# First keys through two queues, half of their blocks on ScalarE, zero rows late, new orders of steps

## What is computed

```python
# layer 0: attention, 32 query heads over 8 key/value heads of depth 8; keys and values are the context itself
x = x + softmax(heads(norm(x)) @ heads(ctx).T / sqrt(8)) @ heads(ctx)
# layer 0: two experts of 1024, the likelier one's output times its probability
h = norm(x) @ w_fc[e].T;  x = x + p[e] * (square(where(h >= 0, h, h / 2)) @ w_proj[e].T)
# layer 1: causal attention, 16 heads of depth 16, keys and values expanded from the context
x = x + attention(norm(x) @ Wq.T, ctx @ Wkv.T) @ Wout.T
# layer 1: eight experts of 128 to 512, the two likeliest with gates, one shared expert
h = norm(x) @ down_w;  every expert e: gelu(gelu(h) @ w1 + b1) @ w2 + b2
# an expert that a row did not choose sees a zero row, so its output for zeros is subtracted through the gates
x = x + (sum of gate * expert + 0.1 * shared) @ up_w + gelu(norm(x)) @ core_w + biases
```

## Time and profile before

| | |
|---|---|
| median of 3 runs | 371.69 us (370.42 to 371.99) |
| profiled execution, its time | 371.51 us |
| its span, first to last instruction | 369.5 us |
| mean granted TensorE clock | 0.972 |
| busy: PE, PEld, DVE, ACT, POOL | 91%, 72%, 48%, 38%, 36% |
| loads and stores | 12.61 MB |

### The profile page before, as it was taken

How to read it: one execution, slowest core, us unless ns; L and a number is a source line. 1 busy time by engine, 2 the same in 40 slices (tenths; PEclk the granted TensorE clock), 3 DMA queues, 4 the chain that set the end, 5 groups by cost and what they waited for, 6 DMA issues and landing times.

```text
span 369.5 us, 8414 instructions
## 1 busy us (share of the span) xinstructions
PE 337.8 (91%) x3442; PEld 267.2 (72%) x3442; DVE 177.1 (48%) x478; ACT 141.7 (38%) x319; POOL 134.3 (36%) x177
## 2 busy tenths in 40 slices
PE   0667699999999999999999998999999999988995
PEld 0336486778876788787867886689878968976884
DVE  4763762395853036726092419252775441553132
ACT  3136034511413633264213221454557456443540
POOL 5688645472742434554252536130152000100000
PEclk9996899999999999999999999999999999997998
DMA  7996000000000000000000000000000000000000
GB/s 223 305 393 280 2 0 2 4 0 2 2 2 0 2 4 2 2 2 0 2 1 3 2 1 2 2 2 0 2 28 2 2 30 2 2 0 28 2 0 28
DMA packets 6708, 12.61 MB, mean 34 GB/s; under 512 B 2448, under 2 KB 5008, under 8 KB 5904
## 3 DMA queue, kind: packets, MB, share of 16 engines
q1 hardware_dynamic: 6352, 11.83, 9.3%
q10 hardware_dynamic: 320, 0.26, 0.2%
HBM read 11.04 MB, written 1.05 MB: 33 GB/s over the span
## 4 chain that ended last, share of the span: by engine, by line
PE 80%; DVE 11%; POOL 2%; ACT 2%; issue 2%; DMA 1%; ACTq 1%; DVEq 0%; POOLq 0%
PE Y L1270 28%; PE S L1270 24%; PE H L1270 23%; DVE MN L1062 2%; PE S L1346 2%; DVE MN L1083 1%; DMA KR<-in_ctxT 1%; PE S L1355 1%; PE S L1454 1%; POOL X L931 1%; ACT L829 1%; DVE ACC L1233 1%; POOL Z L892 1%; POOL Z L900 1%; ACTq L693 1%
## 5 line engine op out<-in xcount | busy, mean ns | idle before, releaser
L1270 PE MATMUL H<-XT,WF 128*128 128x256 f32 x256 | 61.2, 384 | 0.0
L1270 PE MATMUL Y<-WP,A 128*128 128x256 f32 x256 | 61.2, 384 | 0.0
L1270 PEld LDWEIGHTS H<-XT,WF 128*128 128x128 f32 x256 | 47.0, 190 | 9.2 <-issue 2.7
L1270 PEld LDWEIGHTS Y<-WP,A 128*128 128x128 f32 x256 | 46.7, 190 | 8.5 <-issue 2.7
L814 ACT ACTIVATE R<-H 128x512 f32<-128x512 f32 x32 | 19.1, 598 | 76.4 <-PE H L1270 75.2
L842 ACT ACTIVATE A<-H,B 128x256 f32<-128x256 f32 x84 | 35.7, 472 | 31.7 <-PE H L1270 26.3
L947 POOL TENSOR_TENSOR A<-R 128x512 f32<-128x512 f32 x32 | 33.6, 1051 | 36.4 <-ACT R L814 19.5
L1270 PEld LDWEIGHTS Y<-W,A 128*128 128x128 f32 x336 | 43.4, 191 | 4.6 <-issue 2.4
L1270 PE MATMUL Y<-W,A 128*128 128x128 f32 x336 | 45.1, 277 | 0.8 <-DVE ACC L1233 0.5
L1270 PE MATMUL H<-GH,W 128*128 128x256 f32 x168 | 42.9, 381 | 0.5 <-ACT GH L831 0.5
L1233 DVE SCALAR_TENSOR_TENSOR ACC<-Y,gate,ACC 128x128 f32<-128x128 f32 x64 | 22.4, 350 | 41.9 <-PE Y L1270 40.5
(11 more groups left out here) (173 smaller groups left out, 498.2 us busy)
## 6 DMA issues: line engine op xcount, KB each, us to landing
W<-in_w SPq DMA_DIRECT2D x2, 1344.0 KB, 10.3
WF<-in_wf SPq DMA_DIRECT2D x2, 1024.0 KB, 11.6
WP<-in_wp SPq DMA_DIRECT2D x2, 1024.0 KB, 13.9
out_dram<-X SPq DMA_DIRECT2D x8, 128.0 KB, 1.7
KR<-in_ctxT SPq DMA_DIRECT2D x4, 192.0 KB, 3.8
X<-in_x SPq DMA_DIRECT2D x1, 512.0 KB, 7.8
X<-in_x SPq DMA_DIRECT2D x2, 128.0 KB, 2.3
KR<-in_ctxT ACTq DMA_DIRECT2D x4, 64.0 KB, 3.2
```

Source lines behind the costliest of these rows:

```text
L1270: return nc.tensor.matmul(o, a, b, start=start, stop=stop, skip_group_check=shared)
```

## The change

- The keys of tiles 0 and 1: places 0 and 1 are issued by SP, right behind X(0); places 2 and 3 by ACT.
- For tiles 0 and 1, POOL writes only the first column half of the key blocks (c = 0); the other half is a new step "a" on ACT, four activations (Copy with a column as scale). scores0 waits for both.
- In ffn1's expert step on DVE, link stays only for the last expert.
- The planner: "z" is held back to 60 us of the plan's time (34 before); other costs and load times are changed, SLACK of POOL goes from 0.361 to 9.209, of ACT from 0.020 to 0.261, SWITCH from 489.77 to 11220.48, CHANGE from 324.38 to 452.22, and all numbers of URGENCY are new, so that all four lists of steps are made anew.

```diff
     "const": ...
-    "attn0": dict(c="pool 2.1", ...
+    "attn0": dict(a="act 1.1", c="pool 2.08", ...
...
-LOADED = {("attn0", "c"): 4.4, ("attn0", "b"): 6.5, ("ffn0", "x"): 11.0, ("ffn0", "u"): 20.0, ("attn1", "kv"): 12.0,
-          ("ffn1", "z"): 34.0, ("ffn1", "r"): 27.0, ("ffn1", "b"): 27.0, ("ffn1", "c"): 37.0, ("attn1", "w"): 24.0}
-LOADED_X = [2.8, 3.6, 7.0, 7.0, 9.5, 9.5, 9.5, 9.5]
+LOADED = {("attn0", "a"): 5.2, ("attn0", "c"): 5.2, ("attn0", "b"): 6.0, ("ffn0", "x"): 13.0, ("ffn0", "u"): 24.0, ("attn1", "kv"): 14.0,
+          ("ffn1", "z"): 60.0, ("ffn1", "r"): 28.0, ("ffn1", "b"): 29.0, ("ffn1", "c"): 37.0, ("attn1", "w"): 26.0}
+LOADED_X = [2.6, 4.9, 7.0, 7.0, 11.5, 11.5, 11.5, 11.5]
...
-SWITCH = 489.77
-CHANGE = 324.38
-SLACK = {"act": 0.020, "dve": 0.532, "pe": 0.030, "pool": 0.361}
+SWITCH = 11220.48
+CHANGE = 452.22
+SLACK = {"act": 0.261, "dve": 0.627, "pe": 0.018, "pool": 9.209}
...
 URGENCY = {
...
+    "attn0": "a -258 108; k 621 -85 -832 -922 -999 -809 -992 -999; t 746 682 727 771 330 999 150 384; "
+             "c -886 -999 69 -494 -652 -63 460 -751; v -862 -900 -947 -964 -992 -982 -900 -657; "
+             "ln 999 999 217 999 -433 -256 -794 -999; q -445 638 326 614 649 -539 658 658; "
...
+             "n -656 -161 -94 870 999 606 931 951; h 636 -167 702 201 709 -610 -55 -346; "
...
+    "ffn0": "v -476 745 641 779; ln 971 980 907 115; x 907 904 907 974; r 698 727 395 -457; g 116 930 963 32; "
+             "u -903 -978 -669 248; d -999 -987 -987 -968; y -999 -999 -911 -813",
...
+    if (s[0], s[2]) == ("attn0", "c") and s[1] < 2:
+        parts = [(e, d / 2) for e, d in parts]
...
-        def keys(eng, k):
+        def keys(eng, k, places=range(4)):
...
-            for r in range(4):
+            for r in places:
...
             rows(0, 1)
+            keys(sp, 0, (0, 1))
             rows(1, 2)
...
+            def key_blocks0(t, _):
+
+                if t == 0:
+                    act.wait_ge(places_ready, 1)
+                    act.wait_ge(ld_k[0], 16 * 4)
+                for i in range(4):
+                    nc.scalar.activation(Z0[:, t % 2, 1, i, :], KR0[:, 1, t * P:(t + 1) * P], ACT.Copy, scale=quarter0[:, i:i + 1]
+                                         ).then_inc(kz_half, 1)
...
-            keys(act, 0)
+            keys(act, 0, (2, 3))
...
-                for c in range(DC):
+                for c in range(DC if t >= 2 else 1):
                     nc.gpsimd.tensor_tensor(Z0[:, t % 2, c, :, :], ...
...
-                    if k == 0 or j == E1:
+                    if j == E1:
                         link(ins)
...
-                pe.wait_ge(kz_ready, 2 * t + 2)
+                pe.wait_ge(kz_ready, t + 1 if t < 2 else 2 * t)
+                if t < 2:
+                    pe.wait_ge(kz_half, 4 * t + 4)
```

More of the change, by code:

```diff
@@ L74 @@
 COST = {
[L75 to L78, removed]
+    "const": dict(e="dve 1.7 act .9", i="pool 1.4", m="pool 5.0", g="pool 1.6"),
+    "attn0": dict(a="act 1.1", c="pool 2.08", v="dve .83 pool .56", ln="dve .52", q="pe .22 act .37", s="pe 1.06", h="dve .69",
+                  k="pool 2.08", m="dve .6", t="pe .06 dve 1.2", p="pe 1.6", f="act .6", b="act .45", o="pe 1.05", u="act .38",
+                  n="pe .45 dve .82 pool .88"),
     "attn1": dict(kv="pe .97 act .76", c="pool 2.1", v="dve .83 pool .55", ln="dve .41",
                   x="pe .22 act .37", w="pe .89 act .37", s="pe 1.58", h="dve .69", k="pool 2.1",
-                  m="dve .38", t="pe .06 dve 1.2", p="pe 1.4", f="act .6", o="pe .67", u="act .37", n="pe .45 dve .71",
+                  m="dve .45", t="pe .06 dve 1.2", p="pe 1.58", f="act .6", o="pe .67", u="act .37", n="pe .45 dve .71",
                   a="pe .22 act .37", r="pe .87 dve .42"),
@@ L85 @@
     "ffn1": dict(v="dve 1.53 pool .7", ln="dve .77", x="pe .45 act .59", i="pool 1.43", r="pe .9 dve .59",
-                 e="act .2 dve 2.56", t="act .2 dve 1.1", d="pe .87 act 1.13", g="pe .25 act .3", c="pe .86 act .94",
-                 w="pe .43", y="dve .56", k="pe .25 act .37", o="pe 1.3 dve .42", b="act .22 pool .4", z="dve .3 pe 2.4 act .25")}
+                 e="act .2 dve 3.0", t="act .2 dve 1.1", d="pe .87 act 1.13", g="pe .25 act .3", c="pe .86 act .94",
+                 w="pe .43", y="dve .60", k="pe .25 act .37", o="pe 1.3 dve .42", b="act .22 pool .4", z="dve .3 pe 2.4 act .25")}
 COST = {part: {s: [(e, float(d)) for e, d in zip(text.split()[::2], text.split()[1::2])] for s, text in costs.items()}
@@ L187, in attn0 @@
         add(a("s"), a("c"), a("q"))
+        if t < 2:
+            add(a("a"))
+            need(a("s"), a("a"))
         add(a("k"), a("s"))
@@ L203, in attn0 @@
             need(a("c"), ("const", 0, "e", 0), of=0)
+            need(a("a"), ("const", 0, "e", 0), of=0)
             need(a("b"), ("const", 0, "i", 0))
@@ L628, in mixed_network @@
         kz_ready = sem("kz_ready")
+        kz_half = sem("kz_half")
         qz_ready = sem("qz_ready")
@@ L852, in shared @@
                 nc.scalar.activation(flat(ACC[:, :, :]), b[:, 0:GT], ACT.Copy, scale=0.1).then_inc(done, 1)
-            keys(act, 0)
-            run("act", h | {("attn0", "f"): probs0, ("attn0", "b"): values0, ("const", "e"): places0, ("attn1", "f"): probs1, ("attn1", "kv"): keys1,
+            keys(act, 0, (2, 3))
+            run("act", h | {("attn0", "f"): probs0, ("attn0", "b"): values0, ("attn0", "a"): key_blocks0, ("const", "e"): places0, ("attn1", "f"): probs1, ("attn1", "kv"): keys1,
                      ("ffn0", "g"): exps("ffn0", E0), ("ffn0", "u"): leaky, ("ffn1", "e"): exps("ffn1", E1),
```

## The result

The changed kernel takes 373.57 us (median, 371.78 to 376.56) against 371.14 for the kernel before on the same chip (16 runs each): ratio 1.0076, 95% interval 1.0049 to 1.0103. It is slower by 0.8%; the forecast was 1.4% faster, and the time lies just above the range, whose end was 373.5. The profiled execution took 374.64 us, span 372.5, where the one before had 369.5.

What follows compares the result with a forecast made beforehand. PE bounds the middle (busy 274.9 of 278.5 us), latency the first 48.5 us. Earlier first scores (−2.3) and ramp order (−3), all else 0, took 371.69 to 366.4 us (chance 0.50); range 361 to 373.5.

Steps and rivals of the forecast that it cites:

- The ramp's −5.3 us: Start of the kernel: −2.3 us from earlier first scores and −3 us from the new order, passed on to the end.
- Part 1, keys: First keys on two queues: last landing at 5.0 us instead of 6.83; later loads cost zero, at worst 1.3 us.
- Part 2, halves: Half of the first key blocks on ACT, 1.3 us: first scores near 6.85 instead of 9.14, −2.3 us.
- The near bound: Least gain given for the first scores if the keys land at 5.75: −1.4 us.
- Part 3, order: New order of the ramp brings tile 1's scores and XN earlier: −3 us, bounds 0 and −6.
- the far bound: Most the ramp's order could win, −6 us: 3.9 us at scores(1) and two POOL key products of 1.03 us.
- Part 4, rows for zero inputs: Zero rows moved out of the ramp: FFN starts 5.9 us earlier, 4.7 us paid later; 0, bounds −3.6 to +1.
- Parts 5 and 6: Link removed on DVE: zero; new orders of the middle and tail: 0, bounds −3 and +6 us.
- B: Rival: nothing of the ramp's gain comes through, as ACT's blocks wait or other work sets its end; 371.7 us, chance 0.10.
- C: Rival: POOL starves PE in the FFN stage, unready block products standing before squares; slower, 376.9 us, chance 0.14.
- the marks set for right and wrong: Signs in the profile: keys near 5 us, first scores near 6.9, scores(1) near 12, FFN matmuls some 11 us before 48.5.

Runs made afterwards that it cites:

- r1: Kernel before with only the first keys issued through two queues, orders as before; 371.55 us, ratio 1.0051 to the kernel before.
- r10: Changed kernel with s(0) ahead of q(1), kv(0) and kv(1) behind p(1), context and W_kv loaded ahead of later keys; 374.70 us, 1.0122 of the kernel before.
- r11: r10 with the rows for zero inputs also put back early, in the ramp; 371.57 us, ratio 1.0010 to the kernel before.
- r5: Kernel before with only half of the key blocks of tiles 0 and 1 written by ACT; 369.88 us, ratio 0.9981.
- r2: Kernel before with only the rows for zero inputs moved late on PE and their copy late on ACT; 373.89 us, ratio 1.0108.
- r2b: The same kernel as r2, run again for another profile; one execution, 375.89 us.
- r14: r7 with the rows for zero inputs late on PE and ACT, as in r2; 372.67 us, ratio 1.0101 to the kernel before.
- r12: Kernel before with only the shorter link on DVE; 369.65 us, ratio 1.0001.
- r3: Changed kernel with the rows for zero inputs put back where the kernel before has them; 373.45 us, ratio 1.0075 to the kernel before.
- r4: Changed kernel with kv(0) and kv(1) moved behind p(1) on PE, ACT and POOL; 372.68 us, ratio 1.0087 to the kernel before.
- the first pair: The first runs of r10 (zero rows late) and r11 (zero rows early); 374.70 us and 371.57 us.
- the second pair: The kernels of r10 and r11 run again; 372.20 us (1.0052) and 370.02 us (0.9986 of the kernel before).
- r7: Kernel before with first keys on two queues, context and W_kv loaded ahead of later keys, kv(0) and kv(1) behind p(1); 369.39 us, ratio 0.9974.

## Why the prediction was wrong

Two terms failed. The ramp's −5.3 us did not reach the FFN: XT came 1.2 us later than before. And the rows' move, put at 0, costs some 2 to 3 us where it was measured alone.

**Part 1, keys.** The landing was right and a little better: the last issue at 1.94, there by 4.37 (5.0 forecast, 4.45 without competition). The Trainium skill, "DMA: Bandwidth & Descriptors", section "Issuing engines are not separate DMA queues", says that a second issuer saves only its issue time; by it I had 5.9. The measurement decides: the issue came 0.9 us sooner, and the transfer took 2.3 us instead of 3.9, now that it goes ahead of C. What failed is the price: "Zero; at worst 1.3, where PE already waits for a late weight." The loading of weights on PE did wait for W_kv, 0.40 us in the kernel before, and r1 shows 1.35 us at scores(1). The bound was named; the row that decides it was not looked up.

**Part 2, halves.** Four activations took 1.23 us (1.3 forecast), ready at 5.7 (6.3). The step that failed is from there to the scores: 9.27, not 6.85. Two things were missing: q(1) ahead of s(0) on PE, and DVE's Q at 1.22 us for 0.50 beside POOL. With s(0) ahead of q(1), the first scores start at 7.37 in r10, where Q of tile 0 takes 1.34 us, and at 6.62 in r11, where it takes 0.51: the order was 1.9 us of it, the slow Q 0.75. The −2.3 us became +0.1. (The near bound, with a landing at 5.75, comes out as −1.5 by the prediction's own terms, not −1.4.)

**Part 3, order.** Scores(1) at 14.09 (forecast near 12, with 15.3 as the old distance). The −3 came from POOL's and DVE's queues, and the last 1.6 us ahead of scores(1) at 17.60 were PE's own, kv(0). Of the 3.5 us won there, 3.2 were gone again by XN; on that way stand kv(1) ahead of p(0), the cast of 1.80 us and the 32 matmuls at 2.01 us for 1.12. XN's 2.17 us for 0.74 took 1.4 more. The other term of the far bound, POOL's two products, shows no gain in r5 (0.9939 to 1.0023).

**Part 4, rows for zero inputs.** This is the mis-sized term: 0, bounds −3.6 to +1. The late price was right (4.69, for 4.7), the gain was not. "FFN work starts some 5.9 us earlier" came out as 3.4, and as 4.3 in r2, whose ramp is the old one: r waits 1.0 us for XT and a bank (42.50, where z started at 41.54), a time that z had filled, and r's own eight matmuls take 1.84 us at the low clock for 1.05. And the low clock that "the FFN's matmuls would then pay" was put at the difference of 1.2 us (1.4 with all 42 rows' instructions, 41.54 to 47.61), where the first 16 products alone pay 1.4 us in r2 and 1.9 in r2b. In r2 the late start and the slow products are about equal parts of the 3.0 us by which the lead of 2.9 falls short of 5.9. Measured alone: +2.2 to +3.4 us between medians in three ramps; without the 0.9 us of r2's and r14's placing, +2.2 to +3.1.

**Parts 5 and 6** held: r12 shows no change, and the middle is busy as before.

**Rivals.** B named the right event for the ramp (nothing comes through) and stood at 371.7; none of the rivals had part 4 above +1. C had the sign by another way, and that way did not happen: POOL is busy 35%, its squares waited for PE and ACT, and the middle shows no new idle time. Of the marks set for right and wrong, first scores after 6.9 and the FFN's start (45.19, not some 37) show at once that the ramp's gain is missing.

**Open.** That the two mends work only together (r3 and r4 or r10 alone: nothing; r11: all) is measured; why is not shown. That z must start as soon as XN's first transposes are through does not explain it: from the first transpose to z it is 2.5 us in r3 (40.57 to 43.04) and in r11 (40.45 to 42.92), and the two traces are alike there. Nor is it settled where r10 loses its 2 to 3 us in most executions: in the first pair's traces it is the tail's clock, in the second pair's the gap is not there.

## To carry to other kernels

Before a transfer or a step is moved ahead, look in every in-order queue for what stands next in line behind it: here W_kv, on two queues' worth of issues, and kv on PE decided what earlier keys were worth. Work without inputs from the chain (here 4.7 us of zero rows) can be worth more in the gap where TensorE's clock is low than its time there says: on three of four ramps here the kernel was slower without it there, and the first 16 products behind took 5.1 to 5.6 us at the low clock, where they take 3.7. And cost a move at both places with the clock of each, rather than at one. Where two single traces are compared, read the clock of every stretch first: the tail's alone made some 5 us between two executions of one kernel (r2, r2b).

## What was not expected of the hardware

**VectorE beside GpSimd.** The cast that took 1.80 us (0.50 in the kernel before, 0.20 alone, as in r7 at 40.05) began 0.05 us after the memset and ended 0.05 us after it (15.61, 15.56). Q at 7.29 ended 0.34 us after the product beside it, and XN, two operations of 0.74 us together in the kernel before, took 2.17 from 39.86 on, beside a pair of POOL's query blocks that began at 39.80. Reductions of scores beside the same kind of product kept their 0.64 us each (r7, 9.34 to 11.83). The Trainium skill, "SBUF — State Buffer", section "SBUF: two separate sides", says that the port pair of the two engines is locked for a whole instruction and that only some VectorE operations need it. The traces agree: these three end 0.05 to 0.34 us after GpSimd's instruction does, and r7's reductions did not wait. For the order of steps it means that an operation of 0.20 us on DVE's path took 1.80 here when it came just after a long one on POOL.

**TensorE's clock differs between executions of one list.** r7 and r14 have the same steps up to XN's transposes. The granted clock is back at 1.00 by 26 us in r7, and 0.50 from 22 to 34 us in r14. Two matmuls of kv and 128 for the values in r7:

```profile
25.51 0.59 PE L1280 MATMUL S<-WKV,CT 64*128 64x256 f32 x2
...
26.91 2.11 PE L1280 MATMUL S<-PT,V 64*32 64x128 f32 x128
```

and in r14:

```profile
28.72 1.06 PE L1282 MATMUL S<-WKV,CT 64*128 64x256 f32 x2
...
31.41 3.66 PE L1282 MATMUL S<-PT,V 64*32 64x128 f32 x128
```

XN stands at 41.88 in r14 and at 36.46 in r7. The clock is about half of that: r14's second scores of tile 1 are already 2.7 us behind (24.04, 21.32), mostly by operations on DVE beside POOL's (Q 1.29 us for 0.51, a cast 0.92 for 0.20, the operation behind it 0.99 for 0.23). Of 122 single executions of the kernel before, 120 lie between 366.9 and 373.2 us, with mean clocks of 0.986 to 0.963, so one trace shows a mechanism, and only many runs show whether it pays.
